# A selective-scan block and a mixture of experts: slots of their own for the first two tiles, and the step-size product ahead of B and C

## The chip, the cores and the metric

The kernel runs on one core of a Trainium2 chip. The metric is the device time of one execution in microseconds, the median over the timed runs; lower is better.

## What is computed

A sandwich of two layers over x (2 x 4096 x 256). The first is a Mamba-style block, the second a top-k mixture of experts; the change touches the first alone:

```python
xr = rmsnorm(layernorm(x)) @ W_in;  xs, res = split(xr)
xs = silu(causal_conv4(xs) + conv_b)              # per channel, 512 channels
dt, Bm, Cm = split(xs @ W_x, [512, 528])
dt = softplus(dt @ W_dt)
A_disc = exp(-exp(A_log) * dt[..., None]);  Bx = dt[..., None] * Bm * xs[..., None]
h_t = A_disc_t * h_{t-1} + Bx_t;  y_t = sum_n h_t * C_t      # 16 states per channel
out = (y * silu(res)) @ W_out
x = x + layernorm(x_ln + out);  then x = x + layernorm(experts(layernorm(x)))
```

## The kernel before

**Tiles.** The 8192 positions are 16 tiles of T = 512, tile i from sequence i % 2. A tile has 512 channels x 16 states = 8192 rows of recurrence, which are UNITS = 64 scans of 128 rows (`tensor_tensor_scan`, `L827`, VectorE). Four scans are a quad; 16 scans belong to one block c of 128 channels (DC = 4 blocks).

**What a scan needs.** ScalarE makes the decays `pa` (`decays`, `L683`, an Exp over 512), two scans ahead (AHEAD = 2) in three banks, so it can't run further ahead than three scans. The inputs `bq` of a quad are one product of `rep` with B: the ten quads in VECTOR_QUADS on VectorE (`L813`), the quads 1, 3, 5, 7, 9, 11 on GpSimd (`L935`). After a quad GpSimd multiplies `h` by C (`states`, `L942`) and TensorE sums the states (`sum_states`, `L373`). `rep` is block c of `du` (dt and dt*xs) spread over partitions by 16 DMAs of 128 KB that SP issues (`L305`). It has two buffers, so that block c+2 waits for the quads of block c.

**Preparation of a tile (`prep`).** TensorE transposes x (`L386`), then for m = 0 to 3: input product `L392`, copy to `xsp` (ScalarE `L584`), convolution `L400`, copy with bias to `xs` (`L591`). Then Silu over all of `xs` (`L599`), the B/C product (`L420`, copied to `bc` at `L608`, stored to DRAM and loaded as `c_rep` and `b_rep`), and for each block c the step-size product (dt) `L430`. Softplus of dt is `L616` Abs, `L619` Exp, `L756` (VectorE, "o1", which frees the bank), `L625` Ln, `L632` ("s"), `L761` ("o2") and `L765` ("o3"); `L910` on GpSimd makes dt*xs ("u"). All these products go through the one PSUM bank `pp` in the order of the list USES: the next waits until the last is copied out. The gate products `L411` go through the bank `po`, which s, o2 and the output product use too. Ln covers all four blocks in one instruction of 2048 columns.

**Order.** Every engine runs its own list in order, and a wait in it holds all that stands behind. The list is written as a loop over slots t = 0 to 63, one scan in each; the table PREP names the slot of each step, -16 to 127, relative to the step before the tile's own scans. A tile's preparation begins in slot 48 of the step two before its own and ends in slot 31 of its own. Tile 0 has no step before it: the prologue (slots -16 to 63 without scans) does all of it, and beside it the slots of tile 1 up to -1. It also folds W_x and W_dt into one matrix `w_dtx`: transposes of W_x (`L521`, eight in each of two groups), copies (`L717`), products (`L531`), copies (`L721`). The steps of tiles 0 and 1 are written out, those of 2 to 13 are a loop.

## Time and profile before

| | us |
|---|---|
| median of the timed runs | 2296.67 (2296.19 to 2299.91) |
| profiled execution | 2289.07 |
| its span | 2287.4 |
| outside its span | 1.67 |
| TensorE clock granted, mean | 0.834 |

The span has three parts: the prologue until the first scan, the scans, and the experts. VectorE is busy for most of the middle part. Rows of the page and of the timeline give start, busy time, engine, line, operation, tiles and count; idle time before it, with what ended it, stands in brackets. In a run of one line's instructions the mean of one includes its pipeline, so neighbours start a little closer together than that.

### The profile page before, as it was taken

The numbers are of one execution on the slowest core, as the hardware profiler recorded it, in microseconds if no ns is written. First come the engines' busy times: TensorE is split into PE (matmuls) and PEld (weight loads), VectorE is DVE, ScalarE is ACT, GpSimd is POOL, SyncE is SP. The second block draws the span as 40 slices with busy tenths as digits, with TensorE's granted clock in tenths as the row PEclk, the third lists the DMA queues.
The fourth block names the chain that finished last, engine by engine and source line by source line (L and its number), as shares of the span: only waits on it lengthen the run. The fifth ranks groups of instructions, "written<-read, shape, count | busy, mean of one in ns | idle before, by whom it ended". The sixth has DMA issues, their size and how long they took to land. (4 is left out here: it accounts for less than half of the span.)

```text
span 2287.4 us, 22530 instructions
## 1 busy us (share of the span) xinstructions
PE 1597.8 (70%) x5460; PEld 620.7 (27%) x5460; DVE 1896.8 (83%) x2195; ACT 1357.9 (59%) x2466; POOL 1875.7 (82%) x634
## 2 busy tenths in 40 slices
PE   6677869686868778786868686868687865340960
PEld 2222323232322223232313232313132312020860
DVE  1169999999999999999999999999999999937102
ACT  2356666767675767676767676767676765430211
POOL 0069898989898989898989899999999898930656
PEclk9887979788898979797989797979897976575985
DMA  2094526353444444444435353434353534203942
GB/s 87 20 265 93 128 62 139 75 123 91 111 103 101 112 102 112 101 100 105 103 97 116 83 119 85 113 95 109 92 121 79 123 73 113 56 29 121 328 112 72
DMA packets 135582, 244.15 MB, mean 107 GB/s; under 512 B 26032, under 2 KB 78010, under 8 KB 135472
## 3 DMA queue, kind: packets, MB, share of 16 engines
q1 hardware_dynamic: 129584, 232.79, 41.6%
q0 software_dynamic: 5888, 10.29, 1.9%
q14 instruction: 90, 0.74, 0.1%
q8 instruction: 20, 0.33, 0.1%
HBM read 77.88 MB, written 31.13 MB: 48 GB/s over the span
## 5 line engine op out<-in xcount | busy, mean ns | idle before, releaser
L827 DVE TENSOR_TENSOR_SCAN h<-pa,carry,bq 128x512 f32<-128x512 f32 x1024 | 1250.9, 1266 | 80.2 <-POOL bq L935 36.9
L942 POOL TENSOR_TENSOR h<-h,c_rep 128x2048 f32<-128x2048 f32 x256 | 1157.8, 4536 | 77.2 <-ACT carry L676 77.2
L683 ACT ACTIVATE pa<-rep,neg_a 128x512 f32<-128x512 f32 x1024 | 698.5, 688 | 508.0 <-DVE h L827 502.6
L373 PE MATMUL py<-h,blk 128*32 128x512 f32 x2048 | 338.2, 735 | 325.9 <-POOL h L942 268.4
L935 POOL TENSOR_TENSOR bq<-rep,b_rep 128x2048 f32<-128x2048 f32 x96 | 435.0, 4531 | 44.2 <-DVE h L827 38.3
L813 DVE TENSOR_TENSOR bq<-rep,pb 128x2048 f32<-128x2048 f32 x160 | 361.9, 2262 | 9.1 <-PE pb L439 9.1
L400 PE MATMUL pp<-xsp,w_conv 128*128 128x512 f32 x512 | 261.4, 642 | 12.9 <-ACT xsp L584 12.9
L430 PE MATMUL pp<-xs,w_dtx 128*128 128x512 f32 x512 | 246.7, 621 | 30.4 <-DVE du L756 29.6
L392 PE MATMUL pp<-xnt,w_in 128*128 128x512 f32 x256 | 164.6, 777 | 81.3 <-ACT xs L591 68.2
L373 PEld LDWEIGHTS py<-h,blk 128*32 128x32 f32 x2048 | 44.5, 117 | 528.6 <-POOL h L942 355.4
L430 PEld LDWEIGHTS pp<-xs,w_dtx 128*128 128x128 f32 x512 | 94.7, 196 | 181.6 <-issue 117.6
L400 PEld LDWEIGHTS pp<-xsp,w_conv 128*128 128x128 f32 x512 | 96.4, 201 | 167.6 <-issue 115.5
L411 PE MATMUL po<-xnt,w_in 128*128 128x512 f32 x256 | 129.6, 630 | 12.4 <-ACT gate L596 11.2
L453 PE MATMUL po<-w_out,gate 128*128 128x256 f32 x512 | 124.2, 392 | 4.1 <-DVE z L788 3.3
L756 DVE SCALAR_TENSOR_TENSOR du<-pp,du 128x512 f32<-128x512 f32 x64 | 42.9, 671 | 87.0 <-ACT du L619 86.4
L910 POOL TENSOR_TENSOR du<-du,xs 128x512 f32<-128x512 f32 x64 | 81.2, 1268 | 40.6 <-DVE du L765 40.6
L453 PEld LDWEIGHTS po<-w_out,gate 128*128 128x128 f32 x512 | 96.2, 193 | 51.2 <-issue 33.5
L439 PE MATMUL pb<-bc,sel_b 32*128 32x512 f32 x128 | 100.1, 872 | 14.3 <-DVE bq L813 14.3
L392 PEld LDWEIGHTS pp<-xnt,w_in 128*128 128x128 f32 x256 | 53.4, 231 | 180.7 <-ACT xs L591 107.9
L901 POOL TENSOR_TENSOR rs<-var,mhalf 128x8 f32<-128x8 f32 x16 | 27.0, 1685 | 89.8 <-ACT var L561 89.8
L1199 DVE TENSOR_TENSOR act<-act,pv 128x512 f32<-128x512 f32 x16 | 11.0, 688 | 84.3 <-PE pv L1316 84.3
L591 ACT ACTIVATE xs<-pp,cb 128x512 f32<-128x512 f32 x64 | 43.4, 679 | 56.9 <-PE pp L400 56.8
(159 smaller groups left out, 1757.5 us busy)
## 6 DMA issues: line engine op xcount, KB each, us to landing
rep<-du SPq DMA_DIRECT2D x1024, 128.0 KB, 2.4
c_rep<-bc_scratch SPq DMA_DIRECT2D x64, 256.0 KB, 5.0
combine_scratch<-zeros SPq DMA_DIRECT2D x16, 520.0 KB, 8.0
xt<-in_L_attn_x_dram SPq DMA_DIRECT2D x16, 512.0 KB, 3.4
b_rep<-bc_scratch SPq DMA_DIRECT2D x64, 128.0 KB, 3.5
xo<-in_L_attn_x_dram SPq DMA_DIRECT2D x16, 512.0 KB, 4.6
out_dram<-z SPq DMA_DIRECT2D x16, 512.0 KB, 3.2
hidden_scratch<-late SPq DMA_DIRECT2D x16, 512.0 KB, 3.0
```

Source lines behind the costliest of these rows:

```text
L373: mm = pe.matmul(py[32 * j:32 * j + 32, :], blk[:], h[:, quad % 4, j, :], start=(g == 0), stop=(g == 3), tile_position=(0, 32 * j))
L392: mm = pe.matmul(pp[:], w_in[:, k, m * P:(m + 1) * P], xnt[:, k, :], start=(k == 0), stop=(k == KC - 1))
L400: mm = pe.matmul(pp[:], w_conv[:, m, tap, :], xsp[:, m % 2, tap:tap + T], start=(tap == 0), stop=(tap == TAPS - 1))
L411: mm = pe.matmul(po[:], w_in[:, k, DI + m * P:DI + (m + 1) * P], xnt[:, k, :], start=(k == 0), stop=(k == KC - 1))
L430: mm = pe.matmul(pp[:], w_dtx[:, k, c * P:(c + 1) * P], xs[:, k, :], start=(k == 0), stop=(k == DC - 1))
L439: pe.matmul(pb[:, bank, :], sel_b[b:b + 32, g, :], bc[b:b + 32, :], start=True, stop=True, tile_position=(b, 0)).then_inc(s_brep[n], 1)
L453: mm = pe.matmul(po[:, (s % 2) * DM:(s % 2 + 1) * DM], gate[:, par, k, s * P:(s + 1) * P], w_out[:, k, :], start=(k == 0), stop=(k == DC - 1))
L683: act.activation(pa[:, decay_bank(t), :], rep[:, c % 2, t % 4, 0, :], ACT.Exp, scale=neg_a[:, a_column(t):a_column(t) + 1]).then_inc(s_exp, 1)
L813: v.tensor_tensor(bq[:, quad % 2], rep[:, c % 2, :, 1, :], pb[:, pb_bank, :].unsqueeze(1).broadcast_to((P, 4, T)), ALU.mult).then_inc(s_bd, 1)
L827: v.tensor_tensor_scan(h[:, quad % 4, t % 4, :], pa[:, decay_bank(t), :], bq[:, quad % 2, t % 4, :], carry[:, par, t:t + 1], ALU.mult, ALU ...
L935: pool.tensor_tensor(bq[:, 1], rep[:, c % 2, :, 1, :], b_rep[:, g // 2, :].unsqueeze(1).broadcast_to((P, 4, T)), ALU.mult).then_inc(s_bp, 1)
L942: pool.tensor_tensor(h[:, quad % 4], h[:, quad % 4], c_rep[:, par, quad % 4, :].unsqueeze(1).broadcast_to((P, 4, T)), ALU.mult).then_inc(s ...
```

## The change

- The first two tiles get tables of their own, FIRST and SECOND, chosen by `slots(i)`; the tables are read through `at_slots` on all engines. The loop tiles keep PREP.
- In the prologue tile 1 is no longer prepared. FIRST puts block 0 of tile 0 through softplus, u and rep on its own, block 1 behind it, and leaves block 3's Abs to o1 and the Ln of blocks 2 and 3 to the slots 1, 2 and 13 of tile 0's step. SECOND spreads all of tile 1's preparation over the slots 0 to 59 of tile 0's step.
- Ln is cut: for tile 0 into blocks 0, 1 and 2-3, for tile 1 into 0 and 1-3.
- The fold's eight transposes and products are spread one by one between the input and convolution products. The Exp of A_log comes ahead of the Silu.
- Eight of the 16 DMAs of tile 0's first rep are issued by ScalarE.
- Tile 0's gate products use the `pa` banks instead of `po`.
- For all tiles dt of block 0 goes through `pp` ahead of B/C: `USES`, and in PREP `pe_dt[0]` from (18, 19) to (14, 15), `abs[0]` from 21 to 16, `o1[0]` from 23 to 18, `pe_bc` from (14, 15) to (18, 19), `act_bc` from 17 to 21, `store_bc` from 18 to 22.

```diff
-    pe_bc=(14, 15), act_bc=17, store_bc=18, load_c=19, load_b=60, sel=(58, 55, 111, 115),
+    pe_bc=(18, 19), act_bc=21, store_bc=22, load_c=23, load_b=60, sel=(58, 55, 111, 115),
...
+FIRST = dict(
...
+    ln=((19, 0, 1), (27, 1, 2), (77, 2, DC)), s=(20, 28, 79, 82), o2=(21, 29, 80, 83), o3=(22, 30, 81, 84),
...
+SECOND = dict(
...
+    pe_dt=((29, 30), (35, 36), (39, 40), (42, 43)), abs=(31, 38, 41, 45), exp=(32, 39, 42, 45), o1=(33, 40, 43, 46),
...
-USES = ([("turn", k) for k in range(KC)] + [(name, m) for m in range(DC) for name in ("in", "xs")] + [("bc", 0)]
-        + [("dt", c) for c in range(DC)])
+USES = ([("turn", k) for k in range(KC)] + [(name, m) for m in range(DC) for name in ("in", "xs")]
+        + [("dt", 0), ("bc", 0)] + [("dt", c) for c in range(1, DC)])
...
+        def residual_bank(i, m):
+
+            return pa[:, m % 3, :] if isinstance(i, int) and i == 0 else po[:]
...
-                            for r in range(4):
+                            for r in range(2 if isinstance(i, int) and i == 0 and c == 0 else 4):
...
                 for t in range(FIRST_SLOT, UNITS):
                     prep(t, 0, 0)
-                    prep(t - UNITS, 1, 1)
...
+                                if isinstance(i, int) and i == 1:
+                                    pe.wait_ge(s_dt, DC)
...
+                    if isinstance(i, int) and i == 0 and t == at_slots["rep"][0]:
+                        act.wait_ge(s_dt, 1)
+                        act.wait_ge(s_u, 1)
+                        for r in (2, 3):
+                            for j in range(4):
+                                act.dma_start(rep[32 * r:32 * r + 32, 0, j], du[32 * j:32 * j + 32, 0]).then_inc(d_rep[0], 16)
+                    for at, first, stop in at_slots["ln"]:
+                        if t == at:
+                            act.wait_ge(s_sp, DC * i + stop)
+                            if isinstance(i, int) and i == 1:
+                                act.wait_ge(s_o2, DC)
...
                 act.wait_ge(s_nega, 2)
+                act.wait_ge(s_rese, DC)
```

The instructions as they now stand, at three places. ScalarE between the Silu of tile 0 and the first decays (`L599` Silu, `L616` Abs, `L619` Exp, `L608` bc, `L596` gate), before:

```order
L599 ACTIVATE xs<-xs 128x2048
L724 ACT_TABLE_LOAD
L724 ACTIVATE a_nat<-a_nat 128x64
L608 COPY bc<-pp 32x512
L727 ACTIVATE neg_a<-py 128x64
L616 ACTIVATE du<-pp 128x512
L619 ACTIVATE du<-du 128x512
```

and now (`L645` Silu, `L662` Abs, `L665` Exp, `L680` Ln, `L687` s, `L654` bc, `L642` gate):

```order
L645 ACTIVATE xs<-xs 128x2048
L776 COPY w_dtx<-pb 128x512
L662 ACTIVATE du<-pp 128x512
L665 ACT_TABLE_LOAD
L665 ACTIVATE du<-du 128x512
L680 ACT_TABLE_LOAD
L680 ACTIVATE late<-du 128x512
L687 ACTIVATE po<-du 128x512
L654 COPY bc<-pp 32x512
L782 ACTIVATE neg_a<-py 128x64
L642 COPY gate<-pa 128x512
L671 DMA rep<-du 32x1024 x8
```

The Exp of A_log has left this stretch, block 0 goes on to its Ln at once, and eight DMA issues stand in ScalarE's list. GpSimd from tile 0's u products (`L910`) on, before:

```order
L910 TENSOR_TENSOR du<-du,xs 128x512 x4
L935 TENSOR_TENSOR bq<-rep,b_rep 128x2048
L942 TENSOR_TENSOR h<-h,c_rep 128x2048
L935 TENSOR_TENSOR bq<-rep,b_rep 128x2048
L942 TENSOR_TENSOR h<-h,c_rep 128x2048 x2
L935 TENSOR_TENSOR bq<-rep,b_rep 128x2048
L942 TENSOR_TENSOR h<-h,c_rep 128x2048 x2
L935 TENSOR_TENSOR bq<-rep,b_rep 128x2048
```

and now (`L966` u, `L991` bq, `L998` states):

```order
L966 TENSOR_TENSOR du<-du,xs 128x512 x2
L956 TENSOR_TENSOR rs<-var,mhalf 128x8
L958 TENSOR_TENSOR nm<-mean,rs 128x4
L991 TENSOR_TENSOR bq<-rep,b_rep 128x2048
L998 TENSOR_TENSOR h<-h,c_rep 128x2048
L991 TENSOR_TENSOR bq<-rep,b_rep 128x2048
L998 TENSOR_TENSOR h<-h,c_rep 128x2048 x2
L991 TENSOR_TENSOR bq<-rep,b_rep 128x2048
L998 TENSOR_TENSOR h<-h,c_rep 128x2048
L966 TENSOR_TENSOR du<-du,xs 128x512
L998 TENSOR_TENSOR h<-h,c_rep 128x2048
L966 TENSOR_TENSOR du<-du,xs 128x512
```

Two of the four u products have moved between the states of tile 0. ScalarE in slots 41 to 45 of tile 0's step, now (`L662` and `L665` Abs and Exp of tile 1's blocks 2 and 3, `L610` the normalising of tile 2, `L738` decays):

```order
L662 ACTIVATE du<-pp 128x512
L610 ACTIVATE xt<-xt,nm,rs 128x256 x4
L738 ACTIVATE pa<-rep,neg_a 128x512
L665 ACTIVATE du<-du 128x512
L738 ACTIVATE pa<-rep,neg_a 128x512 x2
L731 COPY carry<-h 128x4
L738 ACTIVATE pa<-rep,neg_a 128x512
L662 ACTIVATE du<-pp 128x512
L665 ACTIVATE du<-du 128x512
```

Before, the Abs of block 2 stood at slot 34 and that of block 3 at slot 40; they now follow each other within four slots.

## Rows read from the trace of the kernel before

**Rows 1.** The page: busy time of engines, and the costliest group.

```profile
PE 1597.8 (70%) x5460; PEld 620.7 (27%) x5460; DVE 1896.8 (83%) x2195; ACT 1357.9 (59%) x2466; POOL 1875.7 (82%) x634
L827 DVE TENSOR_TENSOR_SCAN h<-pa,carry,bq 128x512 f32<-128x512 f32 x1024 | 1250.9, 1266 | 80.2 <-POOL bq L935 36.9
```

**Rows 2.** Timeline, 0 to 70 us: start, busy us, engine, line, tiles [idle before].

```profile
21.19 5.47 PE L400 MATMUL pp<-xsp,w_conv 128*128 128x512 f32 x8 [0.86 <-ACT xsp L584]
...
28.09 0.70 ACT L591 ACTIVATE xs<-pp,cb 128x512 f32<-128x512 f32 x1
28.84 1.98 PE L392 MATMUL pp<-xnt,w_in 128*128 128x512 f32 x4 [1.31 <-ACT xs L591]
...
37.48 1.98 PE L392 MATMUL pp<-xnt,w_in 128*128 128x512 f32 x4 [1.31 <-ACT xs L591]
...
52.07 1.98 PE L392 MATMUL pp<-xnt,w_in 128*128 128x512 f32 x4 [1.26 <-ACT xs L591]
...
65.91 0.69 ACT L591 ACTIVATE xs<-pp,cb 128x512 f32<-128x512 f32 x1
66.62 1.28 ACT L599 ACT_TABLE_LOAD   x1
67.91 1.91 ACT L599 ACTIVATE xs<-xs 128x2048 f32<-128x2048 f32 x1
```

**Rows 3.** Timeline, from tile 0's first dt product to its rep DMAs.

```profile
78.29 3.67 PE L430 MATMUL pp<-xs,w_dtx 128*128 128x512 f32 x8 [0.76 <-ACT bc L608]
...
82.00 0.60 ACT L616 ACTIVATE du<-pp 128x512 f32<-128x512 f32 x1 [3.74 <-PE pp L430]
82.62 0.63 ACT L619 ACTIVATE du<-du 128x512 f32<-128x512 f32 x1
...
104.55 2.06 ACT L565 ACTIVATE xt<-xt,nm,rs 128x256 f32<-128x256 f32 x4
...
110.35 0.70 DVE L761 SCALAR_TENSOR_TENSOR po<-po,late 128x512 f32<-128x512 f32 x1 [4.98 <-ACT po L632]
...
111.85 1.26 POOL L910 TENSOR_TENSOR du<-du,xs 128x512 f32<-128x512 f32 x1 [16.18 <-DVE du L765]
...
113.20 10.27 SPq L305 DMA_DIRECT2D rep<-du  x16
```

**Rows 4.** Stretch of tile 0's second rep: us, PE, PEld, DVE, ACT, POOL, PEclk, DMA share, GB/s.

```profile
125.60:135.70 10.10, 8.55 (x19) 2.97 (x19) 2.29 (x1) 3.30 (x6) 4.52 (x1) 1.00 0.99 216
```

**Rows 5.** Timeline of VectorE in tile 0's step.

```profile
136.66 7.16 DVE L827 TENSOR_TENSOR_SCAN h<-pa,carry,bq 128x512 f32<-128x512 f32 x6 [3.97 <-ACT pa L683]
143.74 2.26 DVE L813 TENSOR_TENSOR bq<-rep,pb 128x2048 f32<-128x2048 f32 x1
145.92 9.62 DVE L827 TENSOR_TENSOR_SCAN h<-pa,carry,bq 128x512 f32<-128x512 f32 x8
...
179.95 2.46 DVE L827 TENSOR_TENSOR_SCAN h<-pa,carry,bq 128x512 f32<-128x512 f32 x2 [0.54 <-issue]
...
208.95 2.46 DVE L827 TENSOR_TENSOR_SCAN h<-pa,carry,bq 128x512 f32<-128x512 f32 x2 [1.71 <-ACT pa L683]
...
246.47 7.16 DVE L827 TENSOR_TENSOR_SCAN h<-pa,carry,bq 128x512 f32<-128x512 f32 x6
```

**Rows 6.** Timeline of GpSimd in tile 0's step.

```profile
148.45 4.53 POOL L935 TENSOR_TENSOR bq<-rep,b_rep 128x2048 f32<-128x2048 f32 x1 [1.47 <-DVE h L827]
...
175.37 4.50 POOL L935 TENSOR_TENSOR bq<-rep,b_rep 128x2048 f32<-128x2048 f32 x1
```

**Rows 7.** Timeline of TensorE after idle time.

```profile
84.03 3.70 PE L430 MATMUL pp<-xs,w_dtx 128*128 128x512 f32 x8 [2.07 <-DVE du L756]
...
289.07 6.37 PE L430 MATMUL pp<-xs,w_dtx 128*128 128x512 f32 x8 [2.90 <-DVE du L756]
```

**Rows 8.** Timeline of a later tile: ScalarE and TensorE about its slots 14 to 17.

```profile
747.59 3.60 PE L420 MATMUL pp<-xs,w_bc 128*32 128x512 f32 x8
...
751.69 0.57 ACT L608 COPY bc<-pp 32x512 f32<-32x512 f32 x1
```

More of the change, by code:

```diff
@@ L66, with slots, logarithms @@
 SPREADS = ((0, 0, 0, 15), (2, 1, 2, 14), (1, 0, 13, 12), (3, 0, 15, 13))
-USES = ([("turn", k) for k in range(KC)] + [(name, m) for m in range(DC) for name in ("in", "xs")] + [("bc", 0)]
-        + [("dt", c) for c in range(DC)])
+USES = ([("turn", k) for k in range(KC)] + [(name, m) for m in range(DC) for name in ("in", "xs")]
+        + [("dt", 0), ("bc", 0)] + [("dt", c) for c in range(1, DC)])
 NU = len(USES)
+def slots(i):
+    if isinstance(i, int) and i < 2:
+        return (FIRST, SECOND)[i]
+    return PREP
+def logarithms(i, c):
+    if isinstance(i, int) and i < 2:
+        return ((1, 2, 3, 3), (4, 5, 5, 5))[i][c]
+    return i + 4
 def use(name, k=0):
@@ L291, in prep @@
                     for c in range(DC):
-                        if t == PREP["rep"][c]:
+                        if t == at_slots["rep"][c]:
                             ready = DC * i + c + 1
@@ L377, in prep @@
                 def prep(t, i, par):
+                    at_slots = slots(i)
                     def bank_free(name, k=0):
@@ L388, in prep @@
                     for m in range(DC):
-                        if t == PREP["pe_in"][m]:
+                        if t == at_slots["pe_in"][m]:
                             bank_free("in", m)
@@ L394, in prep @@
                             mm.then_inc(s_pp, 1)
-                        for n, at in enumerate(PREP["pe_conv"][m]):
+                        for n, at in enumerate(at_slots["pe_conv"][m]):
                             if t == at:
@@ L424, in prep @@
                     for c in range(DC):
-                        for n, at in enumerate(PREP["pe_dt"][c]):
+                        for n, at in enumerate(at_slots["pe_dt"][c]):
                             if t == at:
                                 if n == 0:
+                                    if c == 0:
+                                        pe.wait_ge(s_xs, i + 1)
                                     bank_free("dt", c)
@@ L510, in _ @@
                 for t in range(FIRST_SLOT, UNITS):
-                    if t == PREP["pe_in"][0]:
+                    if t == FIRST["pe_in"][0]:
                         pe.wait_ge(s_win, 1)
-                    if t == PREP["pe_conv"][0][0]:
+                    if t == FIRST["pe_conv"][0][0]:
                         pe.wait_ge(s_win, 2)
-                        pe.wait_ge(d_wx, 16)
-                    for j in range(DC):
-                        if t == PREP["pe_conv"][j // 2][1] + 1:
-                            if j >= 2:
-                                pe.wait_ge(s_wxc, j - 1)
-                            for k in range(DC):
-                                mm = pe.transpose(pa[:, j % 2, k * P:(k + 1) * P], wxs[:, k, j * P:(j + 1) * P], ident[:])
-                            mm.then_inc(s_wxt, 1)
@@ L523, in _ @@
-                    for k in range(DC):
-                        if t == PREP["pe_conv"][2 + k // 2][1] + 1:
-                            if k == 0:
+                    for n in range(2 * DC):
+                        if t == FIRST["pe_in"][n // 2] + (1, 5)[n % 2]:
+                            if n == 0:
+                                pe.wait_ge(d_wx, 16)
+                            if n == DC:
                                 pe.wait_ge(d_wdt, 32)
                                 pe.wait_ge(s_wxc, DC)
-                            if k >= 2:
-                                pe.wait_ge(s_wpc, k - 1)
-                            for j in range(DC):
-                                mm = pe.matmul(pb[:, k % 2, :], wxt[:, j, k * P:(k + 1) * P], wdt[:, j, :],
-                                               start=(j == 0), stop=(j == DC - 1))
-                            mm.then_inc(s_wp, 1)
@@ L534, in _ @@
-                    if t == PREP["pe_bc"][0]:
+                            if n < DC:
+                                if n >= 2:
+                                    pe.wait_ge(s_wxc, n - 1)
+                                for k in range(DC):
+                                    mm = pe.transpose(pa[:, n % 2, k * P:(k + 1) * P], wxs[:, k, n * P:(n + 1) * P], ident[:])
+                                mm.then_inc(s_wxt, 1)
+                            else:
+                                k = n - DC
+                                if k >= 2:
+                                    pe.wait_ge(s_wpc, k - 1)
+                                for j in range(DC):
+                                    mm = pe.matmul(pb[:, k % 2, :], wxt[:, j, k * P:(k + 1) * P], wdt[:, j, :],
+                                                   start=(j == 0), stop=(j == DC - 1))
+                                mm.then_inc(s_wp, 1)
@@ L535, in _ @@
+                    if t == FIRST["pe_bc"][0]:
                         pe.wait_ge(s_nega, 1)
@@ L569, in prep @@
                 def prep(t, i, par):
+                    at_slots = slots(i)
                     def filled(name, k=0):
@@ L751, in prep @@
                 def prep(t, i, par):
+                    at_slots = slots(i)
                     for c in range(DC):
                         n = DC * i + c
-                        if t == PREP["o1"][c]:
+                        if t == at_slots["o1"][c]:
                             v.wait_ge(s_sp, n + 1)
@@ L905, in prep @@
                 def prep(t, i, par):
+                    at_slots = slots(i)
                     for c in range(DC):
-                        if t == PREP["u"][c]:
+                        if t == at_slots["u"][c]:
                             pool.wait_ge(s_dt, DC * i + c + 1)
```

111 lines of the change are left out of this document (60 added, 51 removed).

## Prediction, made before the changed kernel was timed

> **What bounds the kernel now.** I read the page first, then the timeline of the first 300 us engine by engine. The 1024 scans make up 1250.9 of VectorE's 1896.8 busy us, with 80.2 us idle before them; GpSimd, at 1875.7 us, is nearly as full [rows 1]. So once scanning has begun, VectorE sets the end, with GpSimd close behind; what comes before the first scan is added whole. The first scan starts at 136.66 [rows 5]. The reader is to see two things: how long the chain to that scan is, and what tile 0's step costs from there to tile 1's first scan. The row at 246.47 begins two scans before that one; at the pitch of (9.62 - 1.27) / 7 = 1.19 us a scan [rows 5] (a scan alone takes 1.27 [rows 1]), tile 1 starts at 248.85, which makes tile 0's step 112.2 us.
>
> **The first term, the chain to the first scan.** All steps go by starts and durations in the rows.
> (a) To the end of Silu. Before, the copy to xs for m = 0 waits until 28.09, behind transposes and their copies, though the convolution's row ends at 26.66 [rows 2]. Now it starts at 26.7: 1.4 us gained. The block from the second to the third input product takes 37.48 - 28.84 = 8.64 us, of which the same 1.4 us goes. The third block takes 14.59 and the last 13.84 (to the copy at 65.91) [rows 2]; each holds two products of the fold, some 3.5 us each (a dt product of that size takes 3.67 [rows 3]), in front of the next xs. Spread singly, one stands beside the copies between input and convolution, and in the last block one falls behind the xs: I get 12.0 and 8.9 us. Sum 1.4 + 1.4 + 2.6 + 4.9 = 10.3: Silu ends at 59.5, not 69.8.
> (b) To the first dt product. Before it starts at 78.29, behind the Exp of A_log and the B/C product [rows 3]: 8.5 us after Silu. Now only one copy of the fold lies between: start 60.1.
> (c) Block 0. Product 3.7, Abs 0.6, table 1.28, Exp 0.6, table 1.28, Ln 0.6, s 0.6, o2 0.7, o3 0.7, u 1.3 [rows 2, 3] give u at 71.6. ScalarE is later by little: bc waits for o1 and a 3.6 us product, and with the A and gate copies it is at 72.1 when its eight DMAs stand next. The 16 of before took 10.27, so 0.64 each [rows 3]: ScalarE is free at 77.2.
> (d) From there to the first scan ScalarE has Abs, table, Exp, table, Ln, s of block 1, the gate copy, Abs of block 2, the statistics of tile 1 (they wait for o3 and, by my estimate from the lists, for 1.9 us of VectorE), table, Exp, gate, four normalisings of 2.1 in all [rows 3], gate and one decay: 14.45 us. First scan at 91.65; rep has landed at about 85 and hides. The first term is 136.66 - 91.65 = **45.0 us** gained.
> The price of a DMA issued by ScalarE is in no row. The near end is 0.51, the far end twice 0.64, since the 16 engines are already busy for 0.99 of the time during one queue's rep [rows 4] and two queues may halve each other's pace. I take 0.64, the nearest row; the bounds move the first scan by -1.0 and +5.1 us.
>
> **The second term, tile 0's step.** VectorE's work in it, each at its duration less 0.08 of overlap: 64 scans 76.2, ten bq of 2.18 [rows 5] 21.8, five o1 3.0, six pairs of o2 and o3 7.1, three gate products 1.7, statistics 1.6: 111.4 us. (Before it was 108.4 and 3.9 us of stalls: one o1 and two pairs fewer.) So 3.0 us come from the prologue. Then the stalls that I find by following the four lists:
> - Slots 4 to 16, 3.9 us: decay 4 stands behind tile 1's first transpose, which waits for the o1 of block 3 (1.2); decay 12 behind the first convolution (1.3); decay 16 behind the Ln of blocks 2 and 3, and s of block 2 behind that (1.4).
> - Slots 27 to 31, 1.5 us. The two u products moved between GpSimd's states add 2.5 us to its chain from quad 3's bq to quad 7's, which ran unbroken from 148.45 to 179.87 [rows 6] and already ended a wait of scan 28 at 179.95 [rows 5]. ScalarE is as late there, with the last convolution and the gate copies of tile 1.
> - o1 of tile 1's block 0 at slot 33: 2.2 us. Its product waits for Silu at slot 28, which comes late for the reason above, and stands behind a state sum and half behind a gate product.
> - Slots 38 and 39, 2.2 us: the Ln of that block and its s.
> - o1 of block 2 at slot 43: 3.4 us. Its product can't start before VectorE's o1 of block 1 at slot 40. Then follow 3.7 of product, 0.5 of Abs, 2.1 of normalising, a decay and the Exp: 7.5 us, for which VectorE has 4.2 us of scans and a gate product. A further 0.3 in slot 51.
> Sum 13.4 us. All these are at TensorE's full level. After 2.07 us of idle time a dt product took 3.70 us, after 2.90 us it took 6.37 [rows 7], in the half level. The products of blocks 0, 2 and 3 stand after 4.7, 4.7 and 3.4 us of waiting in my lists, so I charge them 3.0, 2.65 and 1.3: 7.0 us. The bound is 0.
> Step of tile 0: 111.4 + 13.4 + 7.0 = 131.8 against 112.2: **19.6 us** lost.
>
> **What costs nothing.** The cut Ln at slots 36 and 48 replaces the one that stopped VectorE for 1.71 at 208.95 [rows 5]; each gap falls on a bq of 2.18 us, its cover, without which 1 us returns. SP: the combine stores are now at about 95 to 117, behind tile 0's second rep as before; rep of block 2 is asked for at 129 and lands at 142, when VectorE wants it. The new waits on residual_copied and dt_ready are behind work already done. In the loop tiles dt of block 0 takes the place of B/C: before, the B/C product from 747.59 took 3.60 us and its copy ran at 751.69 without waiting [rows 8]; now Abs stands there and the product has ended at about 751.2. The margin is 0.5 us, so 0 for 14 tiles, bounds -0.3 and +0.3 a tile, or 4 us in all each way.
>
> **A rule against the trace.** At the first Silu the table load starts at 66.62 and the activation 1.29 us later, and the load starts 0.02 us after the last copy ends [rows 2]. The Trainium skill, ScalarE: Activation LUTs, section What ACT_TABLE_LOAD costs, gives each switch 1.28 us and a drain of 1.38 besides. This trace shows no such drain, so I go by it. By the page the two added loads ahead of the first scan would take 2.8 us more, and the estimate would be 2274.
>
> **The sum.** 45.0 - 19.6 = 25.4 us. The profiled execution's 2289.07 becomes 2263.7; the timed median stood 7.6 above that execution, and I carry this over: 2296.67 - 25.4 = 2271.3.
>
> **The rivals.**
> 1. The stalls hide. If TensorE keeps its full level and the single waits overlap, only the first two items stay, 5.4 us: step 116.8, gain 45.0 - 4.6 = 40.4, time 2256. For it: GpSimd sets slot 28 anyway, and lists followed add up waits. Against: the o1 of block 2 has no cover.
> 2. Two queues share the DMA engines: ScalarE's eight issues take 10.3, gain 20.3, time 2276. For it the share of 0.99 [rows 4]; against it that rep lands only 2 to 3 us after its issue, so the queue isn't deep. The split of rep then does nothing that it is meant to. The Trainium skill, DMA: Bandwidth & Descriptors, section Issuing engines are not separate DMA queues, says that DMAs from several engines interleave on the same 16 engines, which fits this rival and would price it at 2276, as the row does.
> 3. Slower: the loop tiles pay. If the dt product at slot 14 ran in the half level in each, it would last 6.87 - 3.70 = 3.2 longer (6.37 or more [rows 7]); less the 0.5 margin, 2.7 us for each of 14 tiles is 37 us, and the kernel ends at 2308. It decides against the change from 25.4 / 14 = 1.8 us a tile. Against it: TensorE is busy with the output products right before that slot, and the B/C product there ran in 3.60 [rows 8].
>
> **How the numbers follow.** Forecast 0.62 (2263 to 2276: half level at all or none of the three products, and the issue price), rival 1 0.18, rival 2 0.12, rival 3 0.03, something between that ends within 0.2% 0.03, a larger loss in tile 1 that follows from the crowded step 0.02. Time 2271. The range takes in rival 1 and rival 2 with another 5 us: 2256 to 2281. 0.2%, about 4.6 us, is what a measurement of this kernel tells from no change. Faster 0.93, same 0.03, slower 0.04.
>
> **What would show it.** First scan between 90 and 97 in the timeline of VectorE; Silu's end at 59 to 60; eight DMA issues of ScalarE of about 5 us at 72; tile 0's step of 125 to 132 us; stalls before o1 at slots 33 and 43 with rows of dt products above 5 us beside them; steps of later tiles as long as before. A first scan after 100, or later steps longer by 1 us each, would make the prediction wrong; so would a step of under 120 us, on the other side.

## The result and the profile after

The changed kernel takes 2270.42 us, the median of five runs (2268.47 to 2277.77), against 2296.22 (2292.15 to 2299.91, five runs) for the kernel before; the ratio is 0.9897 with a 95% interval of 0.9874 to 0.9921. It is faster by 25.8 us, and the forecast of 2271.0 lies 0.6 us away. Two repeats, each on a chip of its own beside the kernel before, gave 2277.53 against 2300.49 and 2278.47 against 2298.31, ratios 0.9900 and 0.9891: gains of 23.0 and 19.8 us. So the effect is about 20 to 26 us, and that the median fell within 1 us of the forecast is in part luck, as the terms below show.

The profiled execution of the changed kernel took 2269.49 us (span 2267.8), that of before 2289.07: 19.6 us apart. On the page the engines' busy times hardly changed; the answer to the group of [rows 1] is this one, with the o1 group beside it:

```profile
L883 DVE TENSOR_TENSOR_SCAN h<-pa,carry,bq 128x512 f32<-128x512 f32 x1024 | 1256.9, 1274 | 78.7 <-ACT pa L738 41.6
...
L812 DVE SCALAR_TENSOR_TENSOR du<-pp,du 128x512 f32<-128x512 f32 x64 | 43.5, 679 | 78.1 <-ACT du L665 78.1
```

The same 1024 scans, with nearly the same idle time before them (78.7 us against 80.2); what moved is where they start. The timeline of the changed kernel up to its first scan answers [rows 2, 3] (start, duration, engine, line, tiles, idle time before):

```profile
25.92 1.98 PE L430 MATMUL pp<-xnt,w_in 128*128 128x512 f32 x4 [0.34 <-ACT xs L637]
...
33.15 1.98 PE L430 MATMUL pp<-xnt,w_in 128*128 128x512 f32 x4 [0.34 <-ACT xs L637]
...
45.27 1.88 PE L430 MATMUL pp<-xnt,w_in 128*128 128x512 f32 x4
...
54.05 0.69 ACT L637 ACTIVATE xs<-pp,cb 128x512 f32<-128x512 f32 x1 [2.76 <-PE pp L438]
54.76 1.28 ACT L645 ACT_TABLE_LOAD   x1
56.05 1.91 ACT L645 ACTIVATE xs<-xs 128x2048 f32<-128x2048 f32 x1
58.49 3.70 PE L474 MATMUL pp<-xs,w_dtx 128*128 128x512 f32 x8 [1.04 <-ACT w_dtx L776]
...
68.73 1.26 POOL L966 TENSOR_TENSOR du<-du,xs 128x512 f32<-128x512 f32 x1 [58.30 <-DVE du L821]
...
78.12 0.60 ACT L662 ACTIVATE du<-pp 128x512 f32<-128x512 f32 x1 [7.76 <-issue]
...
80.69 0.69 DVE L812 SCALAR_TENSOR_TENSOR du<-pp,du 128x512 f32<-128x512 f32 x1 [12.04 <-ACT du L665]
81.44 6.32 PE L474 MATMUL pp<-xs,w_dtx 128*128 128x512 f32 x8 [4.28 <-DVE du L812]
...
87.79 0.60 ACT L662 ACTIVATE du<-pp 128x512 f32<-128x512 f32 x1 [4.10 <-PE pp L474]
...
94.52 3.63 DVE L883 TENSOR_TENSOR_SCAN h<-pa,carry,bq 128x512 f32<-128x512 f32 x3 [0.80 <-ACT pa L738]
```

Two things in this chain were priced too low by the prediction. ScalarE stood for 7.76 us with no operation, "issue", while it issued its eight DMAs. And the dt product of block 2 took 6.32 us after 4.28 us of idle TensorE, so that ScalarE waited 4.10 for it: the half level (granted clock 0.58 while it ran), met already ahead of the first scan. The two queues of the first rep, from the same timeline (the time is that of issuing the eight DMAs):

```profile
70.08 7.99 ACTq L671 DMA_DIRECT2D rep<-du  x8
70.08 7.98 SPq L343 DMA_DIRECT2D rep<-du  x8
```

In tile 0's step the rows of VectorE with more than 1 us of idle time before them, in the changed kernel, are these (they answer [rows 5]), with the row at which tile 1 starts as the last:

```profile
113.57 2.46 DVE L883 TENSOR_TENSOR_SCAN h<-pa,carry,bq 128x512 f32<-128x512 f32 x2 [1.10 <-ACT pa L738]
...
138.28 3.65 DVE L883 TENSOR_TENSOR_SCAN h<-pa,carry,bq 128x512 f32<-128x512 f32 x3 [3.33 <-ACT pa L738]
...
153.81 1.28 DVE L883 TENSOR_TENSOR_SCAN h<-pa,carry,bq 128x512 f32<-128x512 f32 x1 [1.12 <-ACT pa L738]
...
161.88 0.69 DVE L812 SCALAR_TENSOR_TENSOR du<-pp,du 128x512 f32<-128x512 f32 x1 [4.15 <-ACT du L665]
...
172.51 1.28 DVE L883 TENSOR_TENSOR_SCAN h<-pa,carry,bq 128x512 f32<-128x512 f32 x1 [1.85 <-ACT pa L738]
...
187.26 0.69 DVE L812 SCALAR_TENSOR_TENSOR du<-pp,du 128x512 f32<-128x512 f32 x1 [5.82 <-ACT du L665]
...
194.73 0.69 DVE L812 SCALAR_TENSOR_TENSOR du<-pp,du 128x512 f32<-128x512 f32 x1 [1.04 <-ACT du L665]
...
226.43 7.17 DVE L883 TENSOR_TENSOR_SCAN h<-pa,carry,bq 128x512 f32<-128x512 f32 x6
```

The last row begins two scans before tile 1's first; at 1.19 a scan that is 228.81. The step is 228.81 - 94.52 = 134.3 us, in which VectorE stood for 21.9 us, 18.4 of them in the seven rows above.

### The profile page after: what moved, and what is told of

Read it like the earlier page. It is cut to its first block and busy times, and to the rows that moved or that the text cites. A ratio compares the mean times of both kernels' runs of the same rounds, so it can differ in the third digit from the quotient of the medians.

```text
span 2267.8 us, 22540 instructions
## 1 busy us (share of the span) xinstructions
PE 1603.1 (71%) x5460; PEld 629.2 (28%) x5460; DVE 1898.2 (84%) x2195; ACT 1363.1 (60%) x2475; POOL 1876.1 (83%) x634
## 5 line engine op out<-in xcount | busy, mean ns | idle before, releaser
L883 DVE TENSOR_TENSOR_SCAN h<-pa,carry,bq 128x512 f32<-128x512 f32 x1024 | 1256.9, 1274 | 78.7 <-ACT pa L738 41.6
L998 POOL TENSOR_TENSOR h<-h,c_rep 128x2048 f32<-128x2048 f32 x256 | 1157.7, 4534 | 88.3 <-ACT carry L731 88.3
L738 ACT ACTIVATE pa<-rep,neg_a 128x512 f32<-128x512 f32 x1024 | 695.9, 687 | 468.8 <-DVE h L883 462.8
L410 PE MATMUL py<-h,blk 128*32 128x512 f32 x2048 | 336.7, 732 | 318.9 <-POOL h L998 253.1
L991 POOL TENSOR_TENSOR bq<-rep,b_rep 128x2048 f32<-128x2048 f32 x96 | 435.1, 4533 | 38.1 <-DVE h L883 37.0
L410 PEld LDWEIGHTS py<-h,blk 128*32 128x32 f32 x2048 | 44.5, 117 | 520.8 <-POOL h L998 333.7
L966 POOL TENSOR_TENSOR du<-du,xs 128x512 f32<-128x512 f32 x64 | 81.2, 1270 | 91.8 <-DVE du L821 91.8
L454 PE MATMUL po<-xnt,w_in 128*128 128x512 f32 x240 | 131.4, 674 | 12.1 <-ACT gate L642 12.1
L1388 POOL DMA_INDIRECT rowid<-token_table,entry x16 | 15.4, 961 | 71.9 <-DVE entry L1232 67.3
## 6 DMA issues: line engine op xcount, KB each, us to landing
rep<-du SPq DMA_DIRECT2D x1016, 128.0 KB, 2.4
b_rep<-bc_scratch SPq DMA_DIRECT2D x64, 128.0 KB, 3.5
```

The costliest lines, as they stand in the source:

```text
L410: mm = pe.matmul(py[32 * j:32 * j + 32, :], blk[:], h[:, quad % 4, j, :], start=(g == 0), stop=(g == 3), tile_position=(0, 32 * j))
L454: mm = pe.matmul(residual_bank(i, m), w_in[:, k, DI + m * P:DI + (m + 1) * P], xnt[:, k, :], start=(k == 0), stop=(k == KC - 1))
L738: act.activation(pa[:, decay_bank(t), :], rep[:, c % 2, t % 4, 0, :], ACT.Exp, scale=neg_a[:, a_column(t):a_column(t) + 1]).then_inc(s_exp, 1)
L883: v.tensor_tensor_scan(h[:, quad % 4, t % 4, :], pa[:, decay_bank(t), :], bq[:, quad % 2, t % 4, :], carry[:, par, t:t + 1], ALU.mult, ALU ...
L991: pool.tensor_tensor(bq[:, 1], rep[:, c % 2, :, 1, :], b_rep[:, g // 2, :].unsqueeze(1).broadcast_to((P, 4, T)), ALU.mult).then_inc(s_bp, 1)
L998: pool.tensor_tensor(h[:, quad % 4], h[:, quad % 4], c_rep[:, par, quad % 4, :].unsqueeze(1).broadcast_to((P, 4, T)), ALU.mult).then_inc(s ...
```

## The experiments

Starts of first scans are read from VectorE's timeline of each kernel, as in the prediction; the steps of later tiles from the start of each 64th scan. "Loop stretch" is from tile 1's first scan to the last scan (15 tiles), "tail" from there to the end of the span.

| kernel | first scan | step of tile 0 | tile 1's first scan | loop stretch | tail | time, us |
|---|---|---|---|---|---|---|
| before | 136.7 | 112.2 | 248.9 | 1763.8 | 274.7 | 2289.07 |
| after | 94.5 | 134.3 | 228.8 | 1760.3 | 278.7 | 2269.49 |
| a0_again | 95.0 | 134.4 | 229.4 | 1767.2 | 279.4 | 2277.72 |
| a1_again | 94.6 | 134.2 | 228.8 | 1767.1 | 281.8 | 2279.41 |
| e1, loop tiles in the old order | 94.9 | 134.4 | 229.3 | 1765.9 | 282.3 | 2279.35 |
| e2, swap alone | 132.7 | 112.5 | 245.2 | 1755.5 | 285.7 | 2288.09 |
| e3, fold alone | 123.7 | 112.2 | 235.9 | 1761.3 | 282.6 | 2281.48 |
| e4, all on SyncE | 87.1 | 139.4 | 226.5 | 1755.5 | 280.8 | 2264.56 |
| e5, twelve and four | 88.1 | 139.9 | 228.0 | 1755.7 | 281.6 | 2267.00 |
| e6, Exp beside Abs | 94.0 | 132.5 | 226.5 | 1765.3 | 281.1 | 2274.66 |
| e7, tile 1 later | 94.6 | 127.9 | 222.5 | 1770.2 | 281.8 | 2276.22 |
| e8, tile 0's u earlier | 92.8 | 133.5 | 226.3 | 1755.8 | 285.9 | 2269.69 |
| b1, parts together | 87.8 | 128.0 | 215.8 | 1772.9 | 280.9 | 2271.38 |
| b2, b1 and e8 | 87.7 | 127.2 | 214.9 | 1763.4 | 279.9 | 2259.90 |

All columns, the time too, are those of one profiled execution each; e4 to e8 were timed in that one execution alone. The start of the first Silu, which none of e4 to e8, b1 and b2 touches, lies at 56.05 in the changed kernel and between 55.14 and 56.34 in these, so that about 1 us in a first scan's place is chance.

**a0_again: the changed kernel once more.** No edit.

> The changed kernel again, beside the others. My theory is that its profiled execution gained 19.6 us: 42.1 at the first scan (94.52 against 136.66), less 22.1 in tile 0's step (134.3 against 112.2). The medians differ by 25.8. If the 6 us between is only where the executions fell, the timed difference here lies near 20 to 26 us and the first scan again at 94 to 95. If something else gained 6 us, the profile would show it after tile 1's first scan.

Measured: 2277.53 us (2276.21 to 2279.51), ratio 0.9900 (0.9877 to 0.9922). The first 230 us repeat within 0.6 us. As expected, the first scan is where it was, and the gain of 23.0 us lies between 20 and 26. The loop stretch doesn't repeat: it is 6.9 us longer than in the first profile.

**e1: the old order in tiles 2 to 15.** dt ahead of B and C in the first two tiles alone.

```diff
-    pe_bc=(18, 19), act_bc=21, store_bc=22, load_c=23, load_b=60, sel=(58, 55, 111, 115),
-    pe_dt=((14, 15), (23, 24), (30, 31), (37, 38)), abs=(16, 26, 33, 40), exp=(17, 27, 34, 41), o1=(18, 28, 35, 42),
+    pe_bc=(14, 15), act_bc=17, store_bc=18, load_c=19, load_b=60, sel=(58, 55, 111, 115),
+    pe_dt=((18, 19), (24, 25), (31, 32), (37, 38)), abs=(21, 28, 34, 40), exp=(22, 29, 35, 41), o1=(23, 30, 36, 42),
...
+    return (USES if isinstance(i, int) and i < 2 else LOOP_USES).index((name, k))
```

> Only the order of dt and B/C in tiles 2 to 15 is put back to that of before; tiles 0 and 1 keep the new one. Theory: the order in the loop tiles costs and gives nothing, so the time is that of the changed kernel within 4 us and the steps of tiles 1 to 15 are as long. Rival: it was worth something there, at 1 us a tile 14 us, in either direction.

Measured: 2278.26 us, ratio 0.9897 (0.9874 to 0.9921), no difference from a0_again, timed beside it, as expected. By the profiles the old order's loop stretch is 1765.9, 5.6 us more than in the first profile of the changed kernel, and 1.3 less than in a0_again. The new order thus has more than one length; the last part of this section comes back to that.

**e2: the swap alone, on the kernel before.**

```diff
-        + [("dt", c) for c in range(DC)])
+        + [("dt", 0), ("bc", 0)] + [("dt", c) for c in range(1, DC)])
```

> The kernel before with dt of block 0 ahead of B/C for all tiles and nothing else. Theory: in the prologue the dt chain of block 0 no longer waits for the B/C product, but the Ln still waits for all four blocks, and the loop tiles are neutral: within 4 us of before, first scan at 134 to 138. Rival: the swap is a large part of the gain, 10 us or more faster.

Measured: 2293.92 against 2300.49 us, ratio 0.9978 (0.9961 to 0.9996). First scan 4.0 us earlier (132.7, where 134 to 138 was expected), and in this one execution a loop stretch of 1755.5, 8.3 us less than before: 0.6 us a tile. The time was expected within 4 us of before and is 6.6 us under it; the gain in the loop was forecast at 0.

**e3: the fold in single pieces alone**, with the Exp of A_log at its early place.

```diff
-                    for k in range(DC):
-                        if t == PREP["pe_conv"][2 + k // 2][1] + 1:
...
+                    for n in range(2 * DC):
+                        if t == PREP["pe_in"][n // 2] + (1, 5)[n % 2]:
...
-                    if t == PREP["silu_x"] + 1:
+                    if t == PREP["pe_in"][0] + 4:
                         act.wait_ge(d_alog, 16)
                         act.activation(a_nat[:], a_nat[:], ACT.Exp).then_inc(s_nega, 1)
```

> The kernel before with the fold's transposes and products one by one and the Exp of A_log ahead of the Silu, and nothing else. Theory: Silu ends some 11 to 12 us earlier (in the changed kernel it ended at 57.96 against 69.82), the table load of the Exp of A_log goes (1.3), and all of it reaches the first scan, at 123 to 125, and the end: 11 to 14 us faster than before. Rival: the chain to the first scan is held by rep, Ln or tile 1's work, and less than 5 us arrive.

Measured: 2286.64 us, ratio 0.9941 (0.9919 to 0.9964), first scan 13.0 us earlier and the step unchanged, as expected. This sets the parts of the change against each other. Of the 42.1 us by which the first scan moved, the swap and the fold give 17.0, at almost no cost in the step, and tile 1's first scan comes 3.6 and 12.9 us earlier: 16.6 of the 20.1 us that the whole change gains there. The other 25.1 us at the first scan come with the rest, block 0 brought to its scans alone and tile 1 taken out of the prologue, and nearly all the 22.1 us that the step grows go against them: about 3 to 4 us are left. The medians say the same: 6.6 and 13.9 us for the two parts, 23.0 for the whole change beside them. That rest was not run by itself, so its share is a difference and takes it that the parts add up.

**e4 and e5: the split of the first rep.** All sixteen DMAs on SyncE, or twelve there and four on ScalarE.

```diff
-                            for r in range(2 if isinstance(i, int) and i == 0 and c == 0 else 4):
+                            for r in range(4):
...
-                    if isinstance(i, int) and i == 0 and t == at_slots["rep"][0]:
-                        act.wait_ge(s_dt, 1)
-                        act.wait_ge(s_u, 1)
-                        for r in (2, 3):
-                            for j in range(4):
-                                act.dma_start(rep[32 * r:32 * r + 32, 0, j], du[32 * j:32 * j + 32, 0]).then_inc(d_rep[0], 16)
```

> The changed kernel with all 16 DMAs of tile 0's first rep on SP. Theory: the eight issues hold ScalarE for 8.0 us (70.08 to 78.07), which is on the chain. Without them Abs of block 1 goes at 73.6 when its product is ready, the first scan at 88 to 90; but b_rep is loaded 2.3 us later, so that scan 4 waits for GpSimd's first bq until about 98.6, and tile 1's first scan gains only 2 us (226 to 228). Rival: the split is worth its price, the first scan comes no earlier than 94, since rep lands later.

> 12 of the 16 rep DMAs on SP, 4 on ScalarE. Theory: while both queues issue, each needs 1.0 us a DMA, so ScalarE is held for 4.0 us and the first scan comes 4 to 6 us earlier (88 to 91), the dt product of block 2 in the full level since TensorE waits less. Rival (issue time is fixed by the total of 16): ScalarE is held for about 8 us all the same and the first scan stays at 94.

Measured: 2264.56 and 2267.0 us, one execution each, with first scans at 87.09 and 88.12. The timeline of e4:

```profile
55.14 1.91 ACT L645 ACTIVATE xs<-xs 128x2048 f32<-128x2048 f32 x1
...
69.16 10.25 SPq L343 DMA_DIRECT2D rep<-du  x16
...
76.17 3.70 PE L474 MATMUL pp<-xs,w_dtx 128*128 128x512 f32 x8
...
87.09 3.63 DVE L877 TENSOR_TENSOR_SCAN h<-pa,carry,bq 128x512 f32<-128x512 f32 x3 [0.81 <-ACT pa L732]
...
91.60 4.51 POOL L985 TENSOR_TENSOR bq<-rep,b_rep 128x2048 f32<-128x2048 f32 x1 [8.18 <-DMA b_rep<-bc_scratch]
```

Sixteen DMAs take 10.25 us to issue on one queue and 8.0 on two. To the landing of the last one it is 12.2 us from the first issue on one queue and 11.1 on two (landed at 81.32 and at 81.20; 12.2 to 12.5 in e4, b1 and b2, and 11.1 to 11.9 in five executions with eight on each queue), so that the split gains about 1 us of landing, for which nobody waits, and holds ScalarE for 8 us on the path to the first scan. Without it the first scan comes 7.4 us earlier; 0.9 of that stands already at the Silu, which the edit doesn't touch. The dt product of block 2, at 76.17, has no idle time before it now and takes 3.70 us, not 6.32: that half level, too, came with the split. In e5, whose Silu starts at 56.05 as in the changed kernel, ScalarE is held for 3.56 us, this product takes 3.70 as well, and the first scan is 6.4 us earlier. At tile 1's first scan only 2.3 us are left in e4 and 0.8 in e5, since GpSimd's first bq then waits 8.18 us (7.78 in e5) for b_rep, where it waits 0.94 in the changed kernel. A wait behind the removed one took most of the gain.

**e6 and e7: tile 1's places.** In e6 the Exp of block 2 moves from slot 42 to 41, beside its Abs. In e7 tile 1's dt, B/C and logarithms stand in later slots:

```diff
-    pe_dt=((29, 30), (35, 36), (39, 40), (42, 43)), abs=(31, 38, 41, 45), exp=(32, 39, 42, 45), o1=(33, 40, 43, 46),
+    pe_dt=((29, 30), (37, 38), (42, 43), (46, 47)), abs=(33, 40, 45, 49), exp=(33, 40, 45, 49), o1=(34, 41, 46, 50),
...
```

> One number changed: the Exp of tile 1's block 2 at slot 41 and not 42, so that it runs before tile 2's four normalisings and a decay. Theory: the stall of 5.82 before o1 at slot 43 shrinks by the 2.06 + 0.65 that stood between, to about 3.1, and tile 1's first scan comes 2 to 3 us earlier. Rival: the stall is set by the dt product alone and stays above 5.

> The changed kernel with the slots of tile 1's dt products, Abs, Exp and o1 set one to seven slots later, so that the product of a block has three slots between its start and its Abs. Theory: the two stalls of 4.15 (block 0) and 5.82 (block 2) are a matter of slots; they fall to under 2 each, while the Ln at slot 51 and tile 2's transposes cost 1 to 2 us: tile 1's first scan 4 to 7 us earlier, at 222 to 225. Rival: GpSimd's chain sets the step, and it stays at 228 to 229.

Measured: tile 1's first scan at 226.5 and 222.5, 2.3 and 6.3 us earlier than 228.8. So the waits of VectorE in front of o1 (4.15 and 5.82 in the changed kernel) are a matter of places: the chain of product, Abs, Exp and o1 has more slots in e7, these two waits fall to 1.06 and 1.02 (with a new one of 1.90 a little ahead of the first), and the step falls from 134.3 to 127.9. In e6 the second falls to 3.35, and a new one of 1.85 behind it takes part of that back; its step is 132.5. The whole times, 2274.66 and 2276.22 in one execution each, don't show it, because both executions have long loop stretches.

**e8: the wait that the prediction missed.** Ahead of VectorE's 3.33 us, which end at 138.28, the timeline of the changed kernel shows:

```profile
130.27 1.27 POOL L966 TENSOR_TENSOR du<-du,xs 128x512 f32<-128x512 f32 x1
...
131.63 0.69 ACT L637 ACTIVATE xs<-pp,cb 128x512 f32<-128x512 f32 x1 [4.05 <-POOL du L966]
...
133.03 1.28 ACT L648 ACT_TABLE_LOAD   x1
134.33 1.91 ACT L648 ACTIVATE gate<-gate 128x2048 f32<-128x2048 f32 x1
136.25 1.28 ACT L738 ACT_TABLE_LOAD   x1
```

Tile 1's copy to xs of block 2 overwrites what tile 0's u reads. That u stood in the prologue and now stands in slot 18 on GpSimd, behind a bq and an h product; the copy stands in slot 19. e8 moves the tail of tile 0's blocks 2 and 3 three slots ahead:

```diff
-    ln=((19, 0, 1), (27, 1, 2), (77, 2, DC)), s=(20, 28, 79, 82), o2=(21, 29, 80, 83), o3=(22, 30, 81, 84),
-    u=(23, 31, 82, 85), rep=(24, 40, 84, 95), pe_res=(17, 25, 32, 36), act_res=(24, 29, 36, 42), silu_g=84, keep_r=30)
+    ln=((19, 0, 1), (27, 1, 2), (74, 2, DC)), s=(20, 28, 76, 79), o2=(21, 29, 77, 80), o3=(22, 30, 78, 81),
+    u=(23, 31, 79, 82), rep=(24, 40, 84, 95), pe_res=(17, 25, 32, 36), act_res=(24, 29, 36, 42), silu_g=84, keep_r=30)
```

> The changed kernel with one edit: the tail of tile 0's blocks 2 and 3 (Ln piece, second copy, o2, o3, u) stands three slots earlier in tile 0's step, so that GpSimd makes u of block 2 in slot 15 instead of 18. In the changed kernel VectorE stood for 3.33 us at 138.28 in slot 23, after ScalarE had stood for 4.05 us at 131.63 in front of the copy that fills xs block 2 for tile 1, released by GpSimd's u of tile 0, and had then run the gate's Silu with two table loads (133.03 to 137.5). Theory: that wait costs the 3.33 us. With u earlier ScalarE's wait before this copy is under 1 us, VectorE's stall at slot 23 is under 1 us, and tile 1's first scan starts 2 to 3.5 us earlier than 228.8 (225.3 to 226.8). Rival: the Silu with its two loads, 4.5 us in a row on ScalarE, makes the stall by itself. Then ScalarE's wait goes and VectorE still stands for 2.5 us or more there, and tile 1's first scan stays within 1 us of 228.8. A third way: the time is given back at the next wait of the step, o1 of block 0 (4.15 us in the changed kernel), which then shows 6 us or more.

Measured: the releaser changes, the stall mostly stays. From the timeline of e8:

```profile
128.89 0.69 ACT L637 ACTIVATE xs<-pp,cb 128x512 f32<-128x512 f32 x1 [2.15 <-PE pp L438]
...
135.54 3.65 DVE L883 TENSOR_TENSOR_SCAN h<-pa,carry,bq 128x512 f32<-128x512 f32 x3 [2.63 <-ACT pa L738]
```

The copy now waits 2.15 us for its convolution instead of 4.05 for u, and VectorE stands for 2.63 instead of 3.33. An earlier stall grew, too: the Ln now falls on slot 10 (2.26 us at 114.27, where the changed kernel had 1.10). The step is 0.8 us shorter. The other 1.7 us of tile 1's earlier start (226.3) lie ahead of the first scan, which the edit doesn't touch: 0.8 at the Silu already, 0.2 while ScalarE issued its DMAs, and 0.7 from a dt product of 5.60 instead of 6.32 us. So u was the last to release that copy, and cost about 0.8 us; the stall itself is nearer to the rival, the gate's Silu with two table loads, 4.5 us in a row behind a late copy. That Silu by itself was not moved in any run.

**b1 and b2: the parts together.** b1 has e4 and e7, the store of tile 0's B and C issued by ScalarE behind its own copy, and B loaded ahead of C; b2 adds e8.

```diff
-    pe_bc=(19, 20), act_bc=21, store_bc=25, load_c=26, load_b=27, sel=(28, 29, 111, 115),
+    pe_bc=(19, 20), act_bc=21, store_bc=25, load_c=27, load_b=26, sel=(28, 29, 111, 115),
...
+                        if isinstance(i, int) and i == 0:
+                            act.wait_ge(s_free, NU * i + use("bc") + 1)
+                            act.dma_start(bc_dram[par].rearrange("w g r t -> (w g r) t"), bc[32 * par:32 * par + 32, :]).then_inc(d_bcs, 16)
...
```

> Version built from the runs so far, on the changed kernel: all sixteen replication DMAs of the first block on SyncE (none on ScalarE), the store of tile 0's B and C issued by ScalarE right behind the copy that fills it, the four loads of B ahead of those of C, and tile 1's dt, B and C and logarithms in later slots. From the single changes: first scan at 87 to 88 (87.1 with all DMAs on SyncE), the step of tile 0 130 to 133 (139.4 with all DMAs on SyncE, less 6.4 for the later slots, less 1 to 3 for B's earlier arrival), tile 1's first scan at 217 to 221, 8 to 12 us earlier than in the changed kernel (228.8). If the parts add up, the time is 8 to 12 us under the changed kernel's of this call. Rival: the parts lean on the same wait (GpSimd's first B product, held by the loads of B), and tile 1's first scan stays at 222 or later; then under 6 us.

> The version before it with the tail of tile 0's blocks 2 and 3 three slots earlier, too. If the wait of the copy into xs on tile 0's u costs 3.3 us, it is 2 to 3.5 us under that version; if the gate's Silu alone makes that stall, or the time is given back at tile 1's first dt, it is within 1 us of it.

> The changed kernel itself, beside the two versions. Ratio to the kernel before 0.988 to 0.991; first scan 94.5 to 95.0, tile 1's first scan 228.8 to 229.4. If the slower steps (119.3 to 119.6 in place of 117.6 to 118.3) from some tile on belong to an execution and not to a kernel, the tile from which they begin is another one again, or none.

Measured, all in one series: b1 2268.24 us (2257.19 to 2271.38; ratio to before 0.9854, 0.9829 to 0.9879), b2 2262.39 (2252.36 to 2270.83; 0.9841, 0.9811 to 0.9871), the changed kernel 2278.47 (2264.77 to 2282.13; 0.9891, 0.9862 to 0.9920), before 2298.31. By medians b2 is 16 us under the changed kernel and b1 10, though the intervals of the ratios overlap. The place of tile 1's first scan is firmer: 215.8 and 214.9, 13.0 and 13.9 us earlier than 228.8, where 8 to 12 was expected of b1. By this place b2 is 0.9 us ahead of b1, which is what its rival said; the 5.9 us between their medians lie within the spread. In b1 GpSimd's first bq starts at 85.25 after a wait of 1.15, not 8.18. From e4 and e7 alone tile 1 would start at 226.5 - 6.3 = 220.2; by this sum the other 4.4 us go to B's earlier arrival, most of the 5.1 us by which e4's step was longer. B's order by itself was not run. Between b1 and b2 the copy's wait fell from 4.25 to 0.95 and the step by 0.8 us, as between the changed kernel and e8.

**Why the loop stretch varies.** In e2, e4, e5 and e8 the steps of tiles 1 to 13 are all 117.4 to 118.4 us. In a0_again and a1_again those from tile 7 on are 119.3 to 119.6 (the last tile's apart), in e6 from tile 8, in e7 from tile 5, in b1 from tile 3, in b2 from tile 9, and in the first profile of the changed kernel those of tiles 11 to 13. One execution of one kernel, a1_again, holds both kinds. Its timeline at tile 4 (step 117.8), tile 5 (118.2) and then at tile 8 (119.6): TensorE's first input product, the state sum behind it (`L410`), and VectorE's longer waits:

```profile
583.45 1.98 PE L430 MATMUL pp<-xnt,w_in 128*128 128x512 f32 x4 [1.52 <-ACT xs L637]
585.95 5.02 DVE L883 TENSOR_TENSOR_SCAN h<-pa,carry,bq 128x512 f32<-128x512 f32 x4 [1.53 <-ACT pa L738]
...
659.85 2.46 DVE L883 TENSOR_TENSOR_SCAN h<-pa,carry,bq 128x512 f32<-128x512 f32 x2 [2.29 <-POOL bq L991]
...
701.21 3.63 PE L430 MATMUL pp<-xnt,w_in 128*128 128x512 f32 x4 [2.95 <-ACT xs L637]
...
705.21 1.07 PE L410 MATMUL py<-h,blk 128*32 128x512 f32 x8
...
1056.79 3.78 PE L430 MATMUL pp<-xnt,w_in 128*128 128x512 f32 x4 [2.94 <-ACT xs L637]
1059.29 2.46 DVE L883 TENSOR_TENSOR_SCAN h<-pa,carry,bq 128x512 f32<-128x512 f32 x2 [1.53 <-ACT pa L738]
...
1061.36 1.83 PE L410 MATMUL py<-h,blk 128*32 128x512 f32 x8
...
1062.86 2.46 DVE L883 TENSOR_TENSOR_SCAN h<-pa,carry,bq 128x512 f32<-128x512 f32 x2 [1.12 <-ACT pa L738]
...
1135.03 2.46 DVE L883 TENSOR_TENSOR_SCAN h<-pa,carry,bq 128x512 f32<-128x512 f32 x2 [2.30 <-POOL bq L991]
```

In tile 4 the product at the head of the step takes 1.98 us (granted clock 1.00), in tile 8 it takes 3.78 (0.50), and there VectorE stands for 5.6 us in the step (0.28 and 0.33 in rows not shown) instead of 3.8. That makes up the difference of 1.8 between the steps. But the product alone doesn't make a long step. In tile 5 it has the same 2.95 us of idle time before it and takes 3.63 us, nearly all of it in the half level, and the step is 118.2; the state sum behind it takes 1.07 there and 1.83 (0.56) in tile 8. So it is in all 14 profiles, in tiles 2 to 13: in each of the 52 steps of 119.3 us or more the product took 3.78 and the state sum 1.72 to 1.84, while steps with a product of 3.13 to 3.68 and a state sum of 1.06 to 1.14 were 118.0 to 118.9. A step is long where the half level outlasts the first product. That is read from rows that go together; no edit set it. (Tile 1's step, whose products stand closer together, kept its 117.6 in b1 with 3.78 and 1.94.) The kernels with B and C ahead of dt in the loop have such steps too, one in the profile of before (tile 3), three in e1, none in e3, and leave them again; with dt ahead, once begun, they went on to tile 13 in all seven profiles that have them. It also shows in the whole: in the series of a1_again, executions of the changed kernel with a mean granted clock of 0.834 to 0.837 took 2265 to 2266 us, those at 0.823 to 0.830 2277 to 2282. The kernel before, e1 and e3 never went under 0.828. What starts the longer steps in some executions, and why they then stay, is open. So is the tail: it differs by up to 11 us between executions of kernels that don't differ there.

## Why the prediction was right, point by point

- **Silu's end.** Forecast 59.5, measured 57.96. The third and fourth block took 12.1 and 8.8 us against 12.0 and 8.9. The missing 1.5 is in the first block: its successor starts at 25.92 instead of 28.84, a gain of 2.9 where 1.4 was charged. The first convolution took 4.08 us where its row before has 5.47, which the prediction left as it was.
- **First dt product.** 0.6 us behind Silu in the forecast, 0.5 in the trace.
- **Block 0 to its u.** ScalarE reached its DMAs at 70.08, forecast 72.1, of which 1.5 come from the point before.
- **ScalarE's eight DMAs.** The term was mis-sized: 0.64 each, 5.1 in all, against 1.0 each and 8.0 in all. The chosen row was of one queue, and the near bound of 0.51 stands in no row. The measured value lies in the stated bounds (4.1 to 10.3), about midway to rival 2, so this rival's mechanism, two queues that slow each other, was half real. The Trainium skill, DMA: Bandwidth & Descriptors, section Issuing engines are not separate DMA queues, says that DMAs of several engines interleave on the same 16 engines. The trace agrees: the issuing became 22% shorter with the second queue (8.0 against 10.25 us), and the time to the landing of all sixteen by 9% (11.1 against 12.2), not by half.
- **From the DMAs to the first scan.** 14.45 forecast, 16.45 measured. The step that failed is the missing wait before Abs of block 2: its dt product ran in the half level, 6.32 us where 3.7 was assumed. It hangs on the point before, since the product has no idle time before it and takes 3.70 in e4 and e5. The prediction charged this level to three products of tile 1 and not to one of tile 0. All in all the first scan came at 94.52, not 91.65: 42.1 us gained, not 45.0.
- **No drain at a table load.** The trace after agrees with the one before: table load at 54.76, Silu at 56.05, 1.29 us later. The 1.38 us that the Trainium skill, ScalarE: Activation LUTs, section What ACT_TABLE_LOAD costs, adds for a drain don't show.
- **Tile 0's step.** Forecast 131.8, measured 134.3. Stalls and half level together were forecast at 20.4 and measured at 21.9, VectorE's work at 111.4 and 112.4. By place: slots 4 to 16 3.9 against 3.3; slots 38 and 39 2.2 against 2.3; o1 of block 0 with its half level 5.2 against 4.15; o1 of block 2 6.05 against 5.82; o1 of block 3 1.3 against 1.04. All three dt products charged with the half level had it, or part of it (granted clock 0.55, 0.60 and 0.68 in the three rows). Rival 1, that TensorE keeps its full level, is thereby out:

```profile
151.82 3.55 PE L474 MATMUL pp<-xs,w_dtx 128*128 128x512 f32 x4 [4.60 <-ACT xs L645]
...
177.35 6.15 PE L474 MATMUL pp<-xs,w_dtx 128*128 128x512 f32 x8 [4.88 <-DVE du L812]
...
188.00 5.40 PE L474 MATMUL pp<-xs,w_dtx 128*128 128x512 f32 x8 [3.50 <-DVE du L812]
```

- **Slots 17 to 26.** Forecast 0, measured 3.9. That is the largest single miss: tile 1's copies to xs, late by convolution and u, and the gate's Silu behind them.
- **Slots 27 to 31.** 1.5 us were charged to GpSimd's two u products; 1.1 was measured, released by ScalarE. GpSimd had waits of 2.09 and 1.65 us of its own there, so the reason was wrong, though the size was near.
- **Loop tiles.** Forecast 0, with 4 us each way. The swap gave 8.3 us in e2, and the loop stretch with it lies between 1755.5 and 1772.9 over the executions, against 1763.8 before. The prediction compared the place of one product with its margin, and asked neither how many stalls the whole step has nor on which level its other products run. Rival 3 named the half level in the loop as a danger; it is real, at the first input product and what follows it and not at dt, and costs 1 to 2.2 us a tile where it comes, less than the 2.7 that rival gave. The 6.87 us in that rival's sum stand in no row; with the 6.37 of [rows 7] it would be 2.2 us a tile.
- **The sum.** 42.1 - 22.1 = 20.1 us at tile 1's first scan (248.9 to 228.8) for the forecast 25.4; then 3.5 more in the loop stretch, and 4.0 less in the tail, which makes the 19.6 between the profiles. The profiled execution was forecast at 2263.7 and took 2269.49. The 7.6 us carried over from profile to median were not there after: the changed kernel's median lies 0.9 above its profile. These two errors, 5.8 and 6.7 us, cancelled. The profile of before was a short one: no other execution of that kernel was under 2292, and its tail of 274.7 is the shortest of the 14 profiles. The gain of the medians over all three comparisons, 19.8 to 25.8, holds the forecast of 25.4 at its upper edge.

## What to carry to other kernels

Work that is shortened on the path to the first unit of the bound engine comes out whole at the end: the swap and the fold gave 17.0 us at the first scan and 16.6 at tile 1's. Work that is only moved from there into the first step comes back in it: of the other 25 us some 22 did here. It pays by how it is placed, with as many slots between dependent operations as its chain takes (6 us in e7) and its inputs loaded in time; and look once for each overwritten buffer at who still reads it. Splitting DMAs to a second queue is worth asking only if someone waits for them, and not on an engine that is on the path. And where a median is forecast from one profile, the difference between that profile and the median is noise to be put in the range, not a term to carry over.
